# The node norm after the second aggregation: two staged functions become one with three row buffers

## The chip, the cores and the metric

The kernel runs on one core of one Trainium2 chip. The metric is the device time of one execution in microseconds, the median of several runs. The core has TensorE (PE, with its weight loads PEld), VectorE (DVE), ScalarE (ACT), GpSimd (POOL) and SyncE (SP), which only issues transfers here. DVE, ACT and GpSimd work on tiles of 128 partitions in SBUF; PE writes to PSUM.

## The reference

Four layers over 12500 nodes of 256 features: a graph layer, a feed-forward layer with eight experts, a second graph layer with a batch norm, and an attention that routes to four experts. The change touches the third, between the sum over edges and the attention's first product:

```python
def _L1_gnn_ref(x, A_indices, A_values, A_shape, W, bias, gamma, beta):
    h = jnp.einsum('nd,df->nf', x, W)
    row, col = (A_indices[0], A_indices[1])
    gathered = A_values[:, None] * h[col]
    agg = jax.ops.segment_sum(gathered, row, num_segments=A_shape)
    h = agg + bias
    mean = jnp.mean(h, axis=0)
    var = jnp.mean(jnp.square(h - mean), axis=0)
    h = (h - mean) * jax.lax.rsqrt(var + BN_EPS) * gamma + beta
    return jax.nn.relu(h)
...
    x = x + _L1_gnn_ref(_layernorm(x, axis=-1), edge_index, edge_weight, 12500, L1_gnn_W, L1_gnn_bias, L1_gnn_gamma, L1_gnn_beta)
    x = x + _L1_ffn_ref(_layernorm(x, axis=-1)[None], L1_ffn_W_gat, L1_ffn_att_src, L1_ffn_att_dst, L1_ffn_b_gat, L1_ffn_ln_gamma, L1_ffn_ln_beta, L1_ffn_W1, L1_ffn_b1, L1_ffn_W2, L1_ffn_b2, L1_ffn_edge_index)[0]
```

`_L1_ffn_ref` begins with `x_flat @ W_gat`, a product with 16 columns.

## The kernel before

The nodes are padded to 98 tiles of 128 rows (`TILES`), in 14 groups (`GROUPS`) of seven (`GROUP`); a group is an operand of 128x1792 numbers. The program is a row of stages. Each stage (`Stage`) has its own buffers and semaphores, in it every engine has its own list of instructions, and it ends with a barrier of all engines, so nothing of one stage runs beside another. Within a stage the engines are ordered by semaphores alone. `Chain` makes a DVE instruction wait for the one before it; where a stage is a loop (`Fori`), `hold` computes the awaited value in a register, which adds register instructions (L96) between the others.

After the second aggregation the sums over edges of all nodes lie in SBUF (`agg`). Two functions follow.

`node_statistics` (L1551) finds the mean and variance of each of the 256 features. PE sums the 98 tiles with a matrix of ones into `sum_ps` (L1579 to L1582, the middle ones in a loop), DVE makes the mean (L1615). DVE then writes `agg` minus the mean for a group into one of two buffers `dev` (L1622), ACT squares it in place (L1605), PE sums it into `sq_ps` (L1590), and DVE may use the buffer again when PE is done. Variance, root, reciprocal and the rows `gain` and `offset` follow (L1629 to L1638).

`update_nodes` (L805) with `kind="batch_norm"` makes, for each group, `part` = `agg` times `gain` (L987), plus `offset` (L988), and x + max(`part`, 0) (L989), all on DVE; then the layer norm of each row: `bn_stats` and `bn_aggr` for seven tiles (L992, L993), the root on ACT (L938), the reciprocal (L996), and the normalized rows `f` (L1003). SP loads the old rows x (L848) and stores the new x (L851) and f (L854). For each tile PE transposes f (L902), ACT copies the transposed tile back (L933), PE multiplies it with `gat_w` to 16 columns (L909, L910), and ACT copies them into `heads` (L949). A turn of the loop is two groups, with two buffers each for x and f. PE's list has, for each tile, the transposes and then the product of the same tile:

```python
for c in range(2):
    ins = nc.tensor.transpose(xt_ps[m % 2][:, c, :], src[:, c * P:(c + 1) * P], k.ident[:, :])
ins.then_inc(transposed, 1)
pe.wait_ge(used, used_value)
pe.wait_ge(turned, i * PT + m + 3)
```

SP issues both loads of a turn only after both f of the turn before are stored.

Other stages to which rows below belong: `layer_norm_in` (L148) is the first stage: layer norm of x on DVE (L188, L189, L201), a GpSimd addition of a broadcast row to a group (L208) that starts when the group's f are done, and PE's tail in which the transposes of the next tile precede the product of this one. `update_first` (L1012) is the update after the first aggregation, with the same order on PE; its product has 8 columns (L1082) and begins with a matmul for the bias (L1080); its transposes are L1070. `update_experts` (L1114) has three buffers for x; GpSimd clears a buffer there (L1175) and DVE makes f (L1208). In the experts' stage DVE sorts edges with comparisons of two inputs (L471, L472, L473), and GpSimd copies the payload (L491).

## Time and profile before

| | us |
|---|---|
| median of 3 runs | 8925.62 (8924.4 to 8925.65) |
| the profiled execution's own time | 8919.56 |
| its span | 8917.8 |
| node statistics, first PE instruction to the next stage's first load | 6661.83 to 6774.58 |
| node update, first load to the last ACT copy | 6774.58 to 7076.85 |

The profile gives the start, duration and engine of each instruction, and for an idle engine what ended its wait. Over the whole span PE is busy for 77%, DVE for 54%, ACT for 41%, GpSimd for 58%. Because of the barriers a stage is read by itself: what matters is what its engines do in its own window, and which wait ends last there.

### The profile page before, as it was taken

How to read it: one execution, taken by the hardware profiler on the slowest of the kernel's cores; microseconds unless marked ns; L12 is line 12 of the kernel's file. 1: busy time of each engine (PE TensorE's matmuls, PEld its weight loads, DVE VectorE, ACT ScalarE, POOL GpSimd, SP SyncE). 2: the span in 40 equal slices, each digit the busy share in tenths (PEclk: the TensorE clock that was granted, in tenths of full speed). 3: DMA queues.
4: the chain of work that ended last, by engine and by line, in shares of the span. 5: the costliest groups of instructions: out<-in, count | busy, mean ns of one | idle time of the engine just before them, and what ended most of it. 6: DMA issues, size and time to landing. Idle time of an engine off the chain costs nothing. (4 is left out here: it accounts for less than half of the span.)

```text
span 8917.8 us, 85432 instructions
## 1 busy us (share of the span) xinstructions
PE 6843.4 (77%) x22034; PEld 4303.5 (48%) x22034; DVE 4851.0 (54%) x8553; ACT 3689.7 (41%) x9689; POOL 5150.7 (58%) x4954
## 2 busy tenths in 40 slices
PE   5688888888882999974477777777776499999916
PEld 4333333333371666643233334443444388888815
DVE  5455555555545988717666666666655523232315
ACT  3466666666520222223355555555542133333303
POOL 3677777777705222114377777777760177777760
PEclk8555555555556999987667776666666599999968
DMA  4533333333334111115333333333332422222219
GB/s 139 158 101 100 102 102 101 102 102 101 98 116 135 43 48 52 39 62 159 94 96 97 96 97 97 97 96 96 96 89 83 125 63 69 67 66 65 68 24 343
DMA packets 557882, 865.24 MB, mean 97 GB/s; under 512 B 115953, under 2 KB 422596, under 8 KB 557106
## 3 DMA queue, kind: packets, MB, share of 16 engines
q0 software_dynamic: 210368, 480.82, 20.4%
q1 hardware_dynamic: 347062, 379.21, 12.9%
q8 instruction: 184, 3.01, 0.1%
q14 instruction: 268, 2.20, 0.1%
HBM read 641.91 MB, written 219.29 MB: 97 GB/s over the span
## 5 line engine op out<-in xcount | busy, mean ns | idle before, releaser
L718 PE MATMUL part<-rows,spread 128*128 128x256 f32 x6656 | 3374.5, 620 | 939.4 <-DMA rows<-h,row 313.1
L718 PEld LDWEIGHTS part<-rows,spread 128*128 128x128 f32 x6656 | 1544.9, 283 | 2652.2 <-issue 1732.7
L692 DVE TENSOR_TENSOR agg<-agg,part 128x256 f32 x3328 | 1401.5, 421 | 1762.9 <-PE part L718 1468.1
L675 POOL DMA_INDIRECT rows<-h,row x1664 | 1764.3, 1060 | 535.5 <-issue 494.4
L675 POOL DMA_INDIRECT rows<-f,row x1664 | 1661.7, 999 | 534.7 <-issue 498.1
L743 ACT ACTIVATE spread<-iota,place 128x128 f32<-128x128 f32 x3328 | 1017.8, 388 | 1998.5 <-PE part L718 1811.4
L1743 POOL DMA_INDIRECT rows<-gat,src x1122 | 1086.3, 968 | 341.9 <-issue 341.9
L749 ACT ACTIVATE spread<-spread,weight 128x128 f32<-128x128 f32 x3328 | 1017.4, 388 | 13.6
L1819 PE MATMUL hid_ps<-ft,w 128*128 128x256 f32 x3136 | 714.3, 380 | 18.7 <-ACT hid L1870 10.9
L1829 PE MATMUL y_ps<-w,hid 128*128 128x256 f32 x3136 | 708.7, 379 | 0.0
L1819 PEld LDWEIGHTS hid_ps<-ft,w 128*128 128x128 f32 x3136 | 592.6, 191 | 102.4 <-ACT hid L1870 15.8
L1870 ACT ACTIVATE hid<-hid_ps,b 128x256 f32<-128x256 f32 x784 | 324.1, 472 | 756.2 <-PE hid_ps L1819 755.7
L1829 PEld LDWEIGHTS y_ps<-w,hid 128*128 128x128 f32 x3136 | 595.8, 190 | 81.0
L1967 DVE TENSOR_TENSOR y<-y_ps,b 128x512 f32<-128x512 f32 x196 | 135.6, 692 | 850.8 <-PE y_ps L1829 848.7
L491 POOL COPY spare<-pay 128x1024 f32<-128x1024 f32 x93 | 196.9, 2117 | 694.8 <-DVE pay L478 450.4
L472 DVE TENSOR_TENSOR key<-key 128x1024 f32<-128x1024 f32 x342 | 486.7, 1423 | 5.9
L745 ACT ACTIVATE spread<-spread,ones 128x1024 f32<-128x1024 f32 x416 | 477.7, 1148 | 13.5
L1511 PE MATMUL y_ps<-w2s,hid 128*128 128x256 f32 x2048 | 476.2, 386 | 0.0
L1496 PE MATMUL hid_ps<-xt,w1s 128*128 128x512 f32 x1024 | 446.7, 594 | 3.3 <-DMA b2s<-in_L_ffn_b 3.3
L473 DVE TENSOR_TENSOR key<-key 128x1024 f32<-128x1024 f32 x342 | 419.1, 1225 | 11.7
L1511 PEld LDWEIGHTS y_ps<-w2s,hid 128*128 128x128 f32 x2048 | 378.5, 190 | 88.8 <-issue 32.5
L704 DVE TENSOR_TENSOR hot<-iota,fields 128x1280 bf16<-128x1280 f32 (+1 forms) x205 | 305.6, 1491 | 6.9
(373 smaller groups left out, 6228.1 us busy)
## 6 DMA issues: line engine op xcount, KB each, us to landing
x<-x SPq DMA_DIRECT2D x56, 896.0 KB, 8.9
expert_rows<-y SPq DMA_DIRECT2D x196, 256.0 KB
made<-expert_rows SPq DMA_DIRECT2D x14, 3584.0 KB
rows<-f,row POOLq DMA_INDIRECT x1664, 2.8
rows<-h,row POOLq DMA_INDIRECT x1664, 2.8
f<-f SPq DMA_DIRECT2D x28, 896.0 KB, 4.1
rows<-gat,src POOLq DMA_INDIRECT x1122
xbuf<-zero SPq DMA_DIRECT2D x128, 128.0 KB, 2.6
```

Source lines behind the costliest of these rows:

```text
L472: link(nc.vector.tensor_tensor(b[:, :, 0, :], a[:, :, 0, :], a[:, :, 1, :], ALU.min))
L675: pool.indirect_dma_start(out=rows[:, u, :], out_offset=None, in_=table, in_offset=bass.IndirectOffsetOnAxis(ap=q.row[:, p:p + 1], axis=0) ...
L692: nc.vector.tensor_tensor(sum_t, sum_t, part[:, p % NB, 0:D], ALU.add).then_inc(added, 1)
L718: nc.tensor.matmul(part[:, p % NB, 0:D], spread[:, p % (2 * BANKS), :], rows[:, u, :], start=True, stop=True).then_inc(multiplied, 1)
L743: nc.scalar.activation(spread[:, p % (2 * BANKS), :], k.iota[:, :], ACT.Square, bias=q.place[:, p:p + 1]).then_inc(squared, 1)
L745: nc.scalar.activation(spread[:, h, :], spread[:, h, :], ACT.Relu, scale=-1.0, bias=k.ones[:, 0:1]).then_inc(marked, 1)
L749: nc.scalar.activation(spread[:, p % (2 * BANKS), :], spread[:, p % (2 * BANKS), :], ACT.Copy, scale=q.weight[:, p:p + 1]).then_inc(spread ...
L1496: ins = nc.tensor.matmul(hid_ps[h % HB][:, :], w1s[n][:, c, fc * P:(fc + 1) * P], xt[g % 2][:, c, :], start=c == 0, stop=c == 1)
L1511: ins = nc.tensor.matmul(out, hid[g % 2][:, fc, q * P:(q + 1) * P], w2s[n][:, fc, :], start=False, stop=fc == FC - 1)
L1743: pool.indirect_dma_start(out=rows[b % 3][:, j, :], out_offset=None, in_=table, in_offset=at(src[:, b * B + j:b * B + j + 1])).then_inc(ga ...
L1819: ins = nc.tensor.matmul(hid_ps[m % 3][:, c, :], w1[:, e, d, fc * P:(fc + 1) * P], ft[k2 % 2][:, d, :], start=d == 0, stop=d == 1)
L1829: ins = nc.tensor.matmul(y_ps[n % 2][:, q, :], hid[n % 3][:, fc, q * P:(q + 1) * P], w2[:, n % GEXP, fc, :], start=fc == 0, stop=fc == FC - 1)
```

## The change

`node_statistics` and the batch-norm branch of `update_nodes` are replaced by one stage, `normalize_nodes`. (The named tuples `Routed` and `Normed` go too.)

- First sums: PE sums the tiles of the last seven groups, written out without a loop. DVE adds the first seven groups into one group `partial`, of which PE then sums the seven tiles.
- Centring: DVE adds minus the mean to `agg` in place, all 14 groups with no wait between. ACT squares into two buffers of its own, `square`.
- `offset` is gone: since `agg` is centred, a group's `part` is `agg` times `gain` plus beta. Both operations are GpSimd's now, into two buffers `part`; GpSimd starts group g when the sum of group g-2 is done.
- DVE keeps x + max(`part`, 0), the layer norm and f, and has the sum and moments of group g+1 ahead of the f of group g. The f aren't chained to each other.
- x has three buffers. SP loads the first two groups at the start of the stage, and group g+2 after it has stored x of group g; that load waits until f of group g-1 is done.
- PE has the transposes of tile t+1 ahead of the product of tile t, and ACT the copy of tile t+1 ahead of the result of tile t.
- All loops of these two functions are written out.

Of the removed functions the diff shows only the heads.

```diff
-def update_nodes(nc, k, head, x_old, x_new, f_new, w, width, bias, result):
...
-def node_statistics(nc, k, sums, gain, offset, params):
...
+def normalize_nodes(nc, k, sums, params, x_old, x_new, f_new, w, width, result):
...
+    group = lambda g: sums[:, g * GROUP:(g + 1) * GROUP, :]
+    B, HALVES = 3, GROUPS // 2
...
+        square = [s.sb(f"square{h}", [P, GROUP, D], F32) for h in range(2)]
+        part = [s.sb(f"part{h}", [P, GROUP, D], F32) for h in range(2)]
+        x = [s.sb(f"x{b}", [P, GROUP, D], F32) for b in range(B)]
+        f = [s.sb(f"f{b}", [P, GROUP, D], F32) for b in range(2)]
...
+                def load(g):
+                    if g >= B:
+
+                        sp.wait_ge(normed, (g - B + 1) * GROUP)
+                        sp.wait_ge(x_stored[g % B], g // B * 16)
+                    sp.dma_start(x[g % B][:, :, :], xo[g, :, :, :]).then_inc(loaded[g % B], 16)
+
+                load(0)
+                load(1)
+                for g in range(GROUPS):
+                    sp.wait_ge(summed, g + 1)
+                    sp.dma_start(xn[g, :, :, :], x[g % B][:, :, :]).then_inc(x_stored[g % B], 16)
+                    if g + 2 < GROUPS:
+                        load(g + 2)
+                    sp.wait_ge(normed, (g + 1) * GROUP)
+                    sp.dma_start(fn[g, :, :, :], f[g % 2][:, :, :]).then_inc(f_stored[g % 2], 16)
...
+                pool.wait_ge(weighed, 1)
+                for g in range(GROUPS):
+                    if g >= 2:
+                        pool.wait_ge(summed, g - 1)
+                    nc.gpsimd.tensor_tensor(part[g % 2][:, :, :], group(g), bc(gain[:, :], GROUP, 1), ALU.mult).then_inc(scaled, 1)
+                    pool.wait_ge(scaled, g + 1)
+                    nc.gpsimd.tensor_tensor(part[g % 2][:, :, :], part[g % 2][:, :, :], bc(beta_p[:, :], GROUP, 1), ALU.add).then_inc(parted, 1)
...
+                for t in range(HALVES * GROUP, TILES):
+                    nc.tensor.matmul(out, k.ones[:, :], sums[:, t, :], start=t == HALVES * GROUP, stop=False)
+                pe.wait_ge(added, HALVES - 1)
+                for j in range(GROUP):
+                    ins = nc.tensor.matmul(out, k.ones[:, :], partial[:, j, :], start=False, stop=j == GROUP - 1)
+                ins.then_inc(totalled, 1)
+                pe.wait_ge(masked, 1)
+                for g in range(GROUPS):
+                    pe.wait_ge(squared, g + 1)
+                    for j in range(GROUP):
+                        t = g * GROUP + j
+                        ins = nc.tensor.matmul(sq_ps[:, 0:D], (last if t == TILES - 1 else k.ones)[:, :], square[g % 2][:, j, :],
+                                               start=t == 0, stop=t == TILES - 1)
+                    ins.then_inc(used, 1)
...
+                for t in range(TILES):
+                    if t < TILES - 1:
+                        turn(t + 1)
+                    pe.wait_ge(copied, t + 1)
+                    if t >= 2:
+                        pe.wait_ge(made, t - 1)
+                    for c in range(2):
+                        ins = nc.tensor.matmul(out_ps[t % 2][:, 0:width], xt[t % 2][:, c, :], w[:, c, :], start=c == 0, stop=c == 1)
+                    ins.then_inc(multiplied, 1)
...
+                for g in range(GROUPS):
+                    act.wait_ge(centred, g + 1)
+                    if g >= 2:
+                        act.wait_ge(used, g - 1)
+                    nc.scalar.activation(square[g % 2][:, :, :], group(g), ACT.Square).then_inc(squared, 1)
+                act.wait_ge(all_squared, 1)
...
+                for g in range(1, HALVES):
+                    if g > 1:
+                        dve.wait_ge(added, g - 1)
+                    nc.vector.tensor_tensor(partial[:, :, :], group(0) if g == 1 else partial[:, :, :], group(g), ALU.add).then_inc(added, 1)
+                dve.wait_ge(totalled, 1)
+                dve.wait_ge(params_in, 48)
+                link(nc.vector.tensor_tensor(mean[:, :], mean[:, :], bias_p[:, :], ALU.add))
+                link(nc.vector.tensor_tensor(mean[:, :], bias_p[:, :], mean[:, :], ALU.subtract))
+                for g in range(GROUPS):
+                    nc.vector.tensor_tensor(group(g), group(g), bc(mean[:, :], GROUP, 1), ALU.add).then_inc(centred, 1)
+                dve.wait_ge(used, GROUPS)
+                dve.sem_inc(all_squared, 1)
+                dve.wait_ge(rooted, 1)
+                link(nc.vector.tensor_tensor(gain[:, :], std[:, :], gamma_p[:, :], ALU.mult))
+                dve.sem_inc(weighed, 1)
+                def add(g):
+                    xg = x[g % B][:, :, :]
+                    dve.wait_ge(parted, g + 1)
+                    dve.wait_ge(loaded[g % B], (g // B + 1) * 16)
+                    link(nc.vector.scalar_tensor_tensor(xg, part[g % 2][:, :, :], 0.0, xg, ALU.max, ALU.add))
+                    dve.sem_inc(summed, 1)
+                    for j in range(GROUP):
+                        link(nc.vector.bn_stats(stats[:, j, :], x[g % B][:, j, :]))
+                        link(nc.vector.bn_aggr(mv[:, g % 2, j, :], stats[:, j, :]))
+                    dve.sem_inc(var_done, 1)
+                add(0)
+                for g in range(GROUPS):
+                    if g < GROUPS - 1:
+                        add(g + 1)
+                    dve.wait_ge(std_done, g + 1)
+                    link(nc.vector.reciprocal(rstd[:, g % 2, :], row_std[:, g % 2, :]))
+                    if g >= 2:
+                        dve.wait_ge(turned, (g - 1) * GROUP)
+                        dve.wait_ge(f_stored[g % 2], g // 2 * 16)
+                    for j in range(GROUP):
+                        nc.vector.tensor_scalar(f[g % 2][:, j, :], x[g % B][:, j, :], mv[:, g % 2, j, 0:1], rstd[:, g % 2, j:j + 1],
+                                                ALU.subtract, ALU.mult).then_inc(normed, 1)
...
-                with Stage(nc) as s2:
-                    gain, offset = s2.sb("gain", [P, D], F32), s2.sb("offset", [P, D], F32)
-                    node_statistics(nc, k, agg, gain, offset, (a["L1_gnn_bias"], a["L1_gnn_gamma"], a["L1_gnn_beta"]))
-                    update_nodes(nc, k, Normed(kind="batch_norm", sums=agg, gain=gain, offset=offset), x2, x3, f3,
-                                 k.gat_w, W, None, heads)
+                normalize_nodes(nc, k, agg, (a["L1_gnn_bias"], a["L1_gnn_gamma"], a["L1_gnn_beta"]), x2, x3, f3, k.gat_w, W, heads)
```

DVE in the update, a group in the middle. Before (x0, part and f0 are the buffers of x, of the scaled sums and of f; rows that repeat are left out, as are the register instructions between):

```order
L987 TENSOR_TENSOR part_81796<-agg1_46842,gain_81566 128x1792
L988 TENSOR_TENSOR part_81796<-part_81796,offset_81567 128x1792
L989 SCALAR_TENSOR_TENSOR x0_81792<-part_81796,x0_81792 128x1792
L992 BN_STATS stats_81799<-x0_81792 128x6
L993 BN_AGGR mv_81800<-stats_81799 128x2
...
L996 RECIPROCAL rstd_81802<-std_81801 128x7
L1003 TENSOR_SCALAR f0_81794<-x0_81792,mv_81800,rstd_81802 128x256 x7
```

Now:

```order
L1507 SCALAR_TENSOR_TENSOR x1_81580<-part1_81578,x1_81580 128x1792
L1510 BN_STATS stats_81586<-x1_81580 128x6
L1511 BN_AGGR mv_81587<-stats_81586 128x2
...
L1519 RECIPROCAL rstd_81589<-row_std_81588 128x7
L1524 TENSOR_SCALAR f0_81582<-x0_81579,mv_81587,rstd_81589 128x256 x7
```

The two tensor_tensor have left DVE, and between the sum of group 1 (x1) and the next sum stand the f of group 0. GpSimd, which had one instruction in these two functions, has this row of them now (`last` is the mask for the padding):

```order
L1400 AFFINE_SELECT last_81573<-ones 128x128
L1407 TENSOR_TENSOR part0_81577<-agg1_46842,gain_81569 128x1792
L1409 TENSOR_TENSOR part0_81577<-part0_81577,beta_p_81572 128x1792
L1407 TENSOR_TENSOR part1_81578<-agg1_46842,gain_81569 128x1792
L1409 TENSOR_TENSOR part1_81578<-part1_81578,beta_p_81572 128x1792
```

The moved operations alternate between two buffers, 28 in all. PE at the start of the tail. Before, transposes (`xt_ps`) and products (`tail_ps`) of the same tile alternate:

```order
L902 MATMUL xt_ps0_81803<-ident,f0_81794 128x128 x2
L906 REGISTER_ALU
L909 MATMUL tail_ps0_81805<-gat_w,xt0_81797 128x16
L910 MATMUL tail_ps0_81805<-gat_w,xt0_81797 128x16
L899 REGISTER_ALU
```

Now:

```order
L1434 MATMUL xt_ps1_81593<-ident,f0_81582 128x128 x2
L1445 MATMUL out_ps0_81594<-gat_w,xt0_81584 128x16 x2
L1434 MATMUL xt_ps0_81592<-ident,f0_81582 128x128 x2
L1445 MATMUL out_ps1_81595<-gat_w,xt1_81585 128x16 x2
```

The transposes into one buffer stand ahead of the product from the other.

## Rows read from the trace of the kernel before

**Rows 1.** Windows: us, busy us (x instructions) of each engine, clock, DMA share, GB/s.
```profile
6661.00:6711.00 50.00, 49.17 (x196) 32.98 (x196) 0.00 (x0) 0.00 (x0) 0.29 (x1) 0.95 0.03 8
6852.00:7078.00 226.00, 120.58 (x462) 88.55 (x462) 137.06 (x257) 46.76 (x164) 0.00 (x0) 0.50 0.39 126
```

**Rows 2.** Timeline: start us, us, engine line op out<-in, idle before; the statistics.
```profile
6661.83 1.22 PE L1579 MATMUL sum_ps<-agg,ones 128*128 128x256 f32 x2 [5.07 <-ACTq L1601]
...
6711.28 0.42 DVE L1615 TENSOR_SCALAR mean<-sum_ps 128x256 f32<-128x256 f32 x1 [53.75 <-PE sum_ps L1582]
...
6768.34 0.42 DVE L1629 TENSOR_SCALAR var<-sq_ps 128x256 f32<-128x256 f32 x1 [5.11 <-PE sq_ps L1590]
...
6771.18 0.42 DVE L1633 TENSOR_TENSOR gain<-std,row 128x256 f32<-128x256 f32 x1
6771.64 0.42 DVE L1635 TENSOR_TENSOR mean<-mean,row 128x256 f32<-128x256 f32 x1
```

**Rows 3.** Timeline, squares of the deviations: PE after a pause, PE later, ACT.
```profile
6715.64 8.60 PE L1590 MATMUL sq_ps<-dev,ones 128*128 128x256 f32 x28 [4.50 <-ACT dev L1605]
...
6732.60 6.33 PE L1590 MATMUL sq_ps<-dev,ones 128*128 128x256 f32 x28 [1.01 <-ACT dev L1605]
...
6733.90 1.70 ACT L1605 ACTIVATE dev<-dev 128x1792 f32<-128x1792 f32 x1 [1.34 <-DVE dev L1622]
```

**Rows 4.** Timeline of the node update: two loads awaited, and its last instruction.
```profile
6822.12 2.02 DVE L987 TENSOR_TENSOR part<-agg,gain 128x1792 f32<-128x1792 f32 x1 [8.81 <-DMA x<-x]
...
7031.91 2.03 DVE L987 TENSOR_TENSOR part<-agg,gain 128x1792 f32<-128x1792 f32 x1 [8.87 <-DMA x<-x]
...
7076.67 0.18 ACT L949 ACTIVATE heads<-tail_ps 128x16 f32 x1 [1.27 <-PE tail_ps L910]
```

**Rows 5.** Groups by line, the update: count, busy us, mean ns, idle.
```profile
L989 DVE SCALAR_TENSOR_TENSOR x<-part,x 128x1792 f32<-128x1792 f32 x14 | 28.4, 2025 | 1.5
```

**Rows 6.** Layer norm of the first stage: DVE's timeline; GpSimd's line, ns min/median/max.
```profile
24.60 0.43 DVE L188 BATCH_NORM_STATS2 stats<-agg 128x6 f32<-128x256 f32 x1
...
25.28 0.43 DVE L188 BATCH_NORM_STATS2 stats<-agg 128x6 f32<-128x256 f32 x1
...
105.18 2.35 DVE L201 TENSOR_SCALAR f<-agg,mv,rstd 128x256 f32<-128x256 f32 x7
...
L208 POOL TENSOR_TENSOR agg<-agg,b x14: 3977/3982/3997, 36.3 to 145.6; 128x1792 f32<-128x1792 f32 x14
```

**Rows 7.** Timeline while the experts' stage sorts: DVE with two inputs, GpSimd's copy.
```profile
2904.91 1.23 DVE L471 TENSOR_TENSOR mask<-key 128x1024 uint16<-128x1024 f32 x1
2904.94 2.10 POOL L491 COPY spare<-pay 128x1024 f32<-128x1024 f32 x1 [5.07 <-DVE pay L478]
2906.17 1.94 DVE L472 TENSOR_TENSOR key<-key 128x1024 f32<-128x1024 f32 x1
```

**Rows 8.** Timeline of the second node update: a GpSimd memset meets DVE's f.
```profile
4024.45 1.60 POOL L1175 MEMSET clean<- 128x1792 f32 x1
...
4025.12 3.13 DVE L1208 TENSOR_SCALAR f<-x,mv,rstd 128x256 f32<-128x256 f32 x7
```

**Rows 9.** First node update: PE's timeline for one tile, and a window.
```profile
2467.35 0.67 PE L1070 MATMUL xt_ps<-ident,f 128*128 128x128 f32 x2
2467.94 0.59 PE L1080 MATMUL out_ps<-gate_b,ones 1*128 1x8 f32 x2
2468.47 1.02 PE L1082 MATMUL out_ps<-gate_w,xt 128*128 128x8 f32 x4
2469.34 0.67 PE L1070 MATMUL xt_ps<-ident,f 128*128 128x128 f32 x2
...
2466.00:2640.00 174.00, 174.00 (x699) 143.07 (x699) 81.35 (x267) 51.44 (x187) 0.00 (x0) 0.50 0.41 138
```

**Rows 10.** SP's queue in the node update: a store of f, then two loads.
```profile
6813.44 0.37 SPq L854 DMA_DIRECT2D f<-f  x1
6814.36 1.89 SPq L848 DMA_DIRECT2D x<-x  x2
```

More of the change, by code:

```diff
@@ L38 @@
 Pairs = namedtuple("Pairs", "row place weight tile")
-Routed = namedtuple("Routed", "kind table rows scale")
-Normed = namedtuple("Normed", "kind sums gain offset")
 Tally = namedtuple("Tally", "fields counts words")
@@ L1575, in _ @@
             @block.tensor
             def _(pe):
-                pe.wait_ge(go, 1)
                 out = sum_ps[:, 0:D]
-                nc.tensor.matmul(out, k.ones[:, :], sums[:, 0, :], start=True, stop=False)
-                with pe.Fori(1, TILES - 1) as t:
-                    nc.tensor.matmul(out, k.ones[:, :], sums[:, bass.ds(t, 1), :].rearrange("p o d -> p (o d)"), start=False, stop=False)
-                nc.tensor.matmul(out, k.ones[:, :], sums[:, TILES - 1, :], start=False, stop=True).then_inc(summed, 1)
@@ L1583, in _ @@
-                pe.wait_ge(mask_done, 1)
-                def turn(i, first, end):
-                    for h in range(2):
-                        pe.wait_ge(squared, i * 2 + h + 1)
-                        for j in range(GROUP):
-                            is_last = end and h == 1 and j == GROUP - 1
-                            ins = nc.tensor.matmul(sq_ps[:, 0:D], (last if is_last else k.ones)[:, :], dev[h][:, j, :],
-                                                   start=first and h == 0 and j == 0, stop=is_last)
-                        ins.then_inc(used, 1)
@@ new lines, in _, with root, turn @@
+                act.wait_ge(all_squared, 1)
+                nc.scalar.activation(std[:, :], var[:, :], ACT.Sqrt, bias=k.eps[:, :]).then_inc(rooted, 1)
+                def root(g):
+                    act.wait_ge(var_done, g + 1)
+                    nc.scalar.activation(row_std[:, g % 2, :], mv[:, g % 2, :, 1], ACT.Sqrt, bias=k.eps[:, :]).then_inc(std_done, 1)
+                def turn(t):
+                    act.wait_ge(turned, t + 1)
+                    if t >= 2:
+                        act.wait_ge(multiplied, t - 1)
+                    nc.scalar.activation(xt[t % 2][:, :, :], xt_ps[t % 2][:, :, :], ACT.Copy).then_inc(copied, 1)
@@ new lines, in _ @@
+                root(0)
+                root(1)
+                turn(0)
+                for t in range(TILES):
+                    g, j = t // GROUP, t % GROUP
+                    if t < TILES - 1:
+                        turn(t + 1)
+                    if j == 3 and 2 <= g + 1 < GROUPS:
+                        root(g + 1)
+                    act.wait_ge(multiplied, t + 1)
+                    nc.scalar.activation(result[:, t, :], out_ps[t % 2][:, 0:width], ACT.Copy).then_inc(made, 1)
@@ L1611, in _ @@
                 link = Chain(dve, chain)
-                dve.wait_ge(go, 1)
-                dve.wait_ge(loaded, 48)
-                dve.wait_ge(summed, 1)
-                link(nc.vector.tensor_scalar(mean[:, :], sum_ps[:, 0:D], 1.0 / N, None, ALU.mult))
-                def turn(i, again):
-                    for h in range(2):
-                        if again:
-                            hold(dve, go, used, i * 2 + h - 1)
-                        nc.vector.tensor_tensor(dev[h][:, :, :], sums[:, bass.ds((i * 2 + h) * GROUP, GROUP), :], bc(mean[:, :], GROUP, 1),
-                                                ALU.subtract).then_inc(dev_done, 1)
@@ L1631, in _ @@
-                dve.wait_ge(std_done, 1)
+                dve.sem_inc(all_squared, 1)
+                dve.wait_ge(rooted, 1)
                 link(nc.vector.reciprocal(std[:, :], std[:, :]))
-                link(nc.vector.tensor_tensor(gain[:, :], std[:, :], rows[1][:, :], ALU.mult))
-                link(nc.vector.tensor_tensor(mean[:, :], mean[:, :], rows[0][:, :], ALU.add))
-                link(nc.vector.tensor_tensor(tmp[:, :], rows[0][:, :], mean[:, :], ALU.subtract))
-                link(nc.vector.tensor_tensor(tmp[:, :], tmp[:, :], gain[:, :], ALU.mult))
@@ L1638, in _ @@
-                link(nc.vector.tensor_tensor(offset[:, :], tmp[:, :], rows[2][:, :], ALU.add))
+                link(nc.vector.tensor_tensor(gain[:, :], std[:, :], gamma_p[:, :], ALU.mult))
[10 more added lines that the diff above has]
+                    dve.sem_inc(var_done, 1)
```

236 lines of the change are left out of this document (32 added, 204 removed).

## Prediction

> **What bounds the kernel now.** The change stays inside one stretch of the program, from the start of the node statistics at 6661.8 us to the last copy of the node update at 7076.85 us, 415.0 us of a span of 8917.8. The stages are divided by barriers on all engines, so what ends this stretch earlier ends the kernel earlier, one for one. I first read the windows [rows 1]: in the statistics PE is busy nearly all the time; in the update PE is busy 120.6 of 226 us and DVE 137.1, DMA 0.39: nothing is full, so there a chain of waits is the bound. The timeline gives its dates [rows 2]: first sums from 6661.83 until the mean starts at 6711.28 (49.4 us), squares until 6768.3, and the norm's gain is ready at 6771.60, which I call the hand-over: 109.8 us after the start. From there the update takes 305.2 us: two groups of seven tiles take (7031.91 - 6822.12) / 5 = 42.0 us, in which DVE does all the arithmetic of each group in turn, and sits 8.8 us waiting for rows that are loaded only when both buffers are free [rows 4].
>
> **The statistics.** The first sums were 98 tiles of two passes at 49.4 / 196 = 0.25 us a pass, in a loop. The same passes written out run faster in the squares: 28 of them in 6.33 us, from which I take the last one's 0.38 and a wait of 0.15: 5.80 / 27 = 0.215 us. The first 28 after a pause take 8.60 us, 2.3 more, with the clock still at its lower level [rows 3]. The change leaves 49 tiles and 7 tiles of partial sums, 112 passes: 112 x 0.215 + 2.3 = 26.4 us. DVE's six additions (2.03 us for the shape [rows 5], and 0.04 for the wait: two chained steps of 0.42 us start 0.46 apart [rows 2]) take 12.4 us from the same start and are hidden behind the 49 tiles (21 us). If that cover failed the cost would be small, since only the last 3 us of PE's work wait for them.
> Then DVE makes mean and minus mean (0.15 + three steps of 0.46 = 1.5), centres one group (2.03), ACT squares it (1.70 [rows 3] + 0.05): PE starts at 26.4 + 5.3 = 31.7. Before, DVE waited for PE to free one of two buffers and a pair of groups took 7.3 us; now all centring goes in place without a wait and PE is the bound: 196 x 0.215 + 2.3 + 0.5 of small waits = 44.9, so 76.6. Variance, root, reciprocal and gain take 6771.60 - 6768.34 = 3.3 us as before [rows 2]: hand-over at 80.0 us instead of 109.8, a **gain of 29.8 us**. The bounds are 27 (PE's first start and the in-place centring a little slower) and 32 (no cold start in the first sums).
>
> **The update, by engine.** Four later steps on small rows disappear behind the hand-over, as do a barrier and the first load, which now comes during the statistics. A group then costs:
> DVE: one scalar_tensor_tensor of 128x1792, 2.03 + 0.04; seven pairs of bn_stats and bn_aggr, which follow at 0.68 us in the first stage's layer norm (its chain is written without the register waits) [rows 6], 4.75; reciprocal 0.3; seven f at 2.35 together: 9.45 us.
> GpSimd: multiply and add, both 128x1792. The trace has such an add beside DVE's bn_stats: 3.98 us, 14 times between 3.977 and 3.997 [rows 6]. With a wait between and one before: 8.09 us. No row shows a multiply of two tiles on GpSimd; I take the add's time, since shape and operands are the same; lower bound 3.0, upper bound 6 us.
> PE: the tail for a tile is two transposes and four passes with 16 columns. The update of the first layer has the same pipelined order, 8 columns and one more matmul; there PE is busy for 174.00 of 174 us, with the clock at 0.50, and a tile is transposes 0.59, extra matmul 0.53, four passes 0.87 [rows 9]. Without the extra one 1.46 us a tile, 10.2 us a group; I take the lower clock level, since that stage kept it though PE never paused.
> DMA: f store, x store and the load of the next but one group are now issued together. Three such transfers were issued from 6813.44 on [rows 10]; the second was in place when DVE went on at 6822.12 [rows 4], 8.7 us later, and for the third I add 1.3: about 10 us; the loaded rows are needed one period after the burst.
>
> **Which of them sets the period.** Added one by one none would exceed 10.2. But the trace shows DVE and GpSimd shutting each other out. GpSimd's copy and DVE's comparison with two inputs start 0.03 us apart, the copy lasts 2.10 us, and DVE's next two-input operation lasts 1.94 instead of 1.23: it ends 1.07 us after the copy, which is its 1024 elements with nothing before them [rows 7]. An f that meets a GpSimd memset waits too: a group of f lasts 3.13 us instead of the 2.35 of rows 6 and ends 2.2 us after the memset [rows 8]. bn_stats and bn_aggr aren't held up, nor do they hold up GpSimd [rows 6, 8]. So both of GpSimd's operations exclude the scalar_tensor_tensor and the seven f, and only bn and reciprocal (5.05 us) go beside them. GpSimd may begin part(k+2) only after the sum of group k. Then: 8.09 us of GpSimd with bn under it, f 2.2 after it (they wait some 3 us), then the next sum 2.07: **12.4 us a group**. PE's 10.2 and the loads' 10 lie under it.
> The Trainium skill bears on this in two places. SBUF — State Buffer, section "SBUF: two separate sides", calls the shared port pair "an exclusive lock, not a bandwidth split" for a DVE operation with two SBUF inputs or in its two-port mode against a GpSimd operation that reads SBUF; rows 7 and 8 agree, but no row has a scalar_tensor_tensor against a GpSimd tensor_tensor, and by the rule they exclude each other as well. GPSIMD Engine Reference, section "Engine selection", sends element-wise work to VectorE, which speaks against this change: left on DVE, the two operations would give 9.45 + 4.1 = 13.6 us a group, so by these rows the move still gains 1.2.
>
> **The sum of the update.** Start: GpSimd's first part ends 8.1 us after the hand-over, and nothing makes GpSimd wait before part 1's multiply, so I let the first sum end at 14.1, the second at 24.1 (each held up by one operation), the third at 40.5. Ten periods of 12.4 follow: 164.5. The last sum has no GpSimd work before it: 9.4, so 173.9. PE began group 10 13.3 us before that and then has 28 tiles at 1.46, ending 27.6 after; with the last copy 28.2. Together 202.1 instead of 305.2: a **gain of 103.1 us**. End of the stretch at 80.0 + 202.1 = 282.1 instead of 415.0; in all 132.9, say 133 us. The profiled execution took 8919.6 (span 8917.8, 1.8 around it): 8787 and span 8785. The median lies 6 us above it: 8925.6 - 133 = **8793 us**. All other stages keep code and data.
>
> **Rivals.**
> A. The two-tile operations don't shut each other out after all (or only briefly). Then PE's tail is the bound: the first f at 23.2 us after the hand-over, 98 x 1.46 = 143.1, last copy 0.6: 167 instead of 202, time 8793 - 35 = **8758**. For it: the pairs in question are in no row. Against it: two kinds of pairs that are.
> B. The exclusion costs more: GpSimd's multiply is 6 us instead of 4, or GpSimd gets in between two f and DVE waits twice. Period 14.4, 12 of them count: + 24, **8817**. For it: f are issued without waits, and nothing reserves the port for all seven. Against: GpSimd is out of work by then.
> C. Slower than before. The multiply would have to be so long that it eats all: 133 / 13 = 10.2 us more, so 14.2 us, 3.6 times the add. Up to there GpSimd hides nothing and every microsecond counts 13 times. At 20 us: 8793 + 13 x 16 = **9001**. Only an operation that GpSimd does in a wholly different way would do that; nothing in the rows points to it.
> D. It doesn't do what it says: each sum waits for its load, and stores and load follow each other so slowly that a group takes about the 21 us of before. Then only the statistics and the first load are gained: **8885**, still faster. Against it: the loads have 12.4 us for 10.
>
> **How the numbers follow.** Forecast 8793 (own range 8778 to 8806): 0.60. A 0.17, B 0.18, D 0.02, C 0.02, and 0.01 for no visible change. 8793 is the likeliest case's. The range takes in A and B: 8748 (A with the statistics' best bound and a PE a little faster in the tail) to 8822. About 0.2%, 18 us, is what a measurement of this kernel can tell from no change; every case but C and the last is faster by more: faster 0.97, same 0.01, slower 0.02.
>
> **What would show it.** Statistics: first sums in one run of 26 us, squares without gaps, hand-over near 80 us. Update: scalar_tensor_tensor on DVE at a distance of 12.4 us, GpSimd's operations 3.98 us, the first f of each group starting when GpSimd's add ends, and lasting longer than 0.41. A distance of 10.2 with PE never idle speaks for A, GpSimd operations of 5 us and more for B. The clock in the update at 0.50; were it at 1.0, PE's last 28 tiles would take up to half the time, and the kernel up to 14 us less. The prediction is wrong if the sum waits for its load (DMA x), or if GpSimd's operations don't touch DVE's at all.

## The result and the profile after

| | before | after |
|---|---|---|
| median, us (runs) | 8925.01 (4: 8915.02 to 8925.65) | 8777.52 (4: 8774.87 to 8782.68) |
| ratio, 95% interval | | 0.9837 [0.9825, 0.9849] |
| profiled execution, us (its span) | 8919.6 (8917.8) | 8777.8 (8776.0) |
| mean granted clock of PE | | 0.733 |
| the stretch: start of the statistics to the last copy of the update, us | 415.0 | 275.0 |

The kernel became 147.5 us faster, where 8793 (132.6 faster than the runs shown then) had been predicted; the measured time lies in the range and is 15.5 us below the forecast. Of the 141.8 us between the two spans 140.0 lie in the stretch. The stage starts 2.5 us later than before and what follows it takes 4.3 us less; the code of those parts is the same.

Two other views of the stage, first the windows: us from and to, length, busy us (x instructions) of PE, PE's weight loads, DVE, ACT and GpSimd, granted clock, DMA share, GB/s. The first two answer to the statistics in [rows 1], the third to the update there.

```profile
6662.00:6692.00 30.00, 26.84 (x112) 22.98 (x112) 13.05 (x8) 0.00 (x0) 0.29 (x1) 0.88 0.23 75
6698.00:6741.00 43.00, 42.70 (x194) 37.14 (x192) 22.02 (x13) 20.62 (x13) 0.00 (x0) 0.98 0.00 1
6780.00:6911.00 131.00, 90.77 (x456) 89.58 (x454) 121.94 (x251) 44.92 (x162) 79.38 (x20) 0.50 0.73 226
```

In the squares PE now runs without a gap. In the update PE is busy 91 of 131 us, GpSimd 79 and DVE 122, and DVE's busy time contains its waiting for GpSimd, as the timeline shows below. The DMA share went from 0.39 to 0.73: the same rows in less time.

The timeline of PE in the statistics (start us, us, engine line operation, idle before), which answers to [rows 2, 3]:

```profile
6664.32 23.81 PE L1415 MATMUL sum_ps<-agg,ones 128*128 128x256 f32 x98 [5.10 <-PEq L70]
6687.97 3.19 PE L1418 MATMUL sum_ps<-partial,ones 128*128 128x256 f32 x14
6696.47 43.80 PE L1425 MATMUL sq_ps<-square,ones 128*128 128x256 f32 x194 [5.31 <-ACT square L1454]
```

The first sums are one run of 26.9 us, the partial sums follow without a wait, and the squares are one run of 43.8 us, with two last passes behind it. The gain is ready at 6743.99 (its operation starts at 6743.57 and takes 0.42), 79.7 us after the start.

The timeline of DVE, GpSimd and SP for one period of the update, which has no counterpart before, since there DVE did all of it alone:

```profile
6842.55 2.01 DVE L1507 SCALAR_TENSOR_TENSOR x<-part,x 128x1792 f32<-128x1792 f32 x1
6842.66 0.36 SPq L1391 DMA_DIRECT2D f<-f  x1
6843.06 0.72 SPq L1387 DMA_DIRECT2D x<-x  x1
6843.88 1.39 SPq L1381 DMA_DIRECT2D x<-x  x1
6844.70 3.99 POOL L1407 TENSOR_TENSOR part<-agg,gain 128x1792 f32<-128x1792 f32 x1 [4.16 <-DVEq L1508]
6848.77 3.96 POOL L1409 TENSOR_TENSOR part<-part,beta_p 128x1792 f32<-128x1792 f32 x1
6849.57 0.20 DVE L1519 RECIPROCAL rstd<-row_std 128x7 f32<-128x7 f32 x1
6849.81 5.00 DVE L1524 TENSOR_SCALAR f<-x,mv,rstd 128x256 f32<-128x256 f32 x7
6854.73 2.01 DVE L1507 SCALAR_TENSOR_TENSOR x<-part,x 128x1792 f32<-128x1792 f32 x1
```

GpSimd starts 2.15 us after the sum starts, its two operations end at 6852.73, and the seven f, which take 2.35 us when nothing holds them up, end at 6854.81: 2.08 us after GpSimd. 2.15 + 8.03 + 2.00 (from GpSimd's end to the next sum) = 12.18 us, the distance of the two sums. The answer for the tile f between 6840 and 6870 has the durations of single f (ns, minimum, median, maximum of 21):

```profile
L1524 DVE TENSOR_SCALAR f<-x,mv,rstd x21: 400/403/3065, 6837.6 to 6866.6; 128x256 f32<-128x256 f32 x21
```

One long f of 3.07 us accounts for the whole difference between 5.00 and 2.35, and it is the first of its group: 6849.81 + 3.07 is 6852.88, just behind GpSimd's end at 6852.73. The wait shows as a longer duration, not as a late start.

### The profile page after: what moved, and what is told of

It reads as the page before. It is cut to its first block and busy times, and to the rows that moved or that the text cites. A ratio compares the mean times of both kernels' runs of the same rounds, so it can differ in the third digit from the quotient of the medians.

```text
span 8776.0 us, 83571 instructions
## 1 busy us (share of the span) xinstructions
PE 6792.9 (77%) x21950; PEld 4303.2 (49%) x21950; DVE 4835.4 (55%) x8529; ACT 3686.7 (42%) x9689; POOL 5263.6 (60%) x4982
## 5 line engine op out<-in xcount | busy, mean ns | idle before, releaser
L1287 PEld LDWEIGHTS hid_ps<-xt,w1s 128*128 128x128 f32 x1024 | 195.7, 191 | 234.6 <-issue 233.0
```

What stands on the lines that cost most here:

```text
L1287: ins = nc.tensor.matmul(hid_ps[h % HB][:, :], w1s[n][:, c, fc * P:(fc + 1) * P], xt[g % 2][:, c, :], start=c == 0, stop=c == 1)
```

## The experiments

Dates are counted from the start of the stage. The changed kernel has: hand-over 79.7, first sum starts at 87.9, last at 249.6, end of the stage 275.0; distances of the sums 10.9 and 18.0 at first, then 12.17 to 12.19 with one of 12.8, and 10.45 for the last. The chip of the first four runs took 10344.1 us for the kernel before, with other stages longer, while the durations inside this stage were those above; there I compare stages, not totals. Unless the text says otherwise, the theory in an expectation is that of the prediction.

**dve_scale.** Both scaling operations go back to DVE.

```diff
-                    dve.wait_ge(parted, g + 1)
+                    link(nc.vector.tensor_tensor(part[g % 2][:, :, :], group(g), bc(gain[:, :], GROUP, 1), ALU.mult))
+                    link(nc.vector.tensor_tensor(part[g % 2][:, :, :], part[g % 2][:, :, :], bc(beta_p[:, :], GROUP, 1), ALU.add))
```

> The changed kernel with both scaling operations (agg times gain, plus beta) back on DVE, ahead of the sum; GpSimd has nothing to do in the update. In the changed kernel sums on DVE are 12.18 us apart and the stage lasts 275.0 us from its start to the last ACT copy. Theory (GpSimd and DVE shut each other out, so the move only hides 5 of 8 us under bn_stats and costs the f their place): f takes 2.35 us a group again instead of 5.0, distance 7.1 + 2.35 + 2 x 2.07 = 13.6; the start is 8 us shorter; stage about 284 us. Rival (the loads set the distance of 12.2): distance stays 12.2 and the stage is some 8 us shorter, 267. Rival (the move to GpSimd hides all of its 4.1 us): distance 16.3, stage about 310.

Total 10213.0. Hand-over 80.7, first distance 11.2, then 13.64 to 13.66 with one of 13.9, end 285.5. DVE's timeline of one period:

```profile
7239.53 2.03 DVE L1500 SCALAR_TENSOR_TENSOR x<-part,x 128x1792 f32<-128x1792 f32 x1
...
7246.81 2.35 DVE L1517 TENSOR_SCALAR f<-x,mv,rstd 128x256 f32<-128x256 f32 x7
7249.07 2.03 DVE L1497 TENSOR_TENSOR part<-agg,gain 128x1792 f32<-128x1792 f32 x1
7251.13 2.02 DVE L1498 TENSOR_TENSOR part<-part,beta_p 128x1792 f32<-128x1792 f32 x1
7253.19 2.03 DVE L1500 SCALAR_TENSOR_TENSOR x<-part,x 128x1792 f32<-128x1792 f32 x1
```

With GpSimd silent the seven f take 2.35 us. The move to GpSimd takes 4.1 us of work off DVE in each group but gains only 13.65 - 12.18 = 1.47 a group: the rest goes into the wait of f. At the end of the stage it has gained 10.5 us. At the start it costs 8.0 (the third sum starts 37.1 us after the hand-over instead of 29.1), the later distances bring 17.5, and 1.0 is a later hand-over in this run.

**two_bufs.** x has two buffers instead of three.

```diff
-    B, HALVES = 3, GROUPS // 2
+    B, HALVES = 2, GROUPS // 2
```

> The changed kernel with two buffers of x instead of three, all else the same. A load can then start only when f of the group two before is done, and the next sum waits for it. Theory: the load's 5.3 us comes on top: f done 10.3 us after a sum, load 5.3, sum 2.0, distance 17.6, stage 275 + 11 x 5.4 = 335. Rival (the third buffer hides nothing, since GpSimd sets the distance): distance 12.2, 275. Rival (store and load share the queue, the load takes 10): distance 22, stage 385.

Total 10291.0, distance 18.0 to 19.6 (the third sum comes after 24.2, the last after 15.5), end 348.3: the third buffer is worth 73 us, more than half of what the whole change brings. That is nearest to the theory and 13 us over it, in part because DVE goes on 5.8 to 7.3 us after a load is issued, where 5.3 had been expected. DVE's timeline and SP's:

```profile
...
7266.80 2.03 DVE L1507 SCALAR_TENSOR_TENSOR x<-part,x 128x1792 f32<-128x1792 f32 x1 [5.89 <-DMA x<-x]
```
```profile
7260.93 0.36 SPq L1381 DMA_DIRECT2D x<-x  x1
7261.33 0.56 SPq L1391 DMA_DIRECT2D f<-f  x1
...
```

A group's sum now waits for a load that is issued only when the f before it are done. Here SP issues this load (L1381) ahead of the stores of f and x, and DVE goes on 5.9 us later. I come back to that.

**sums_on_pe.** PE sums all 98 tiles of the first sums, DVE adds nothing.

```diff
-                for t in range(HALVES * GROUP, TILES):
-                    nc.tensor.matmul(out, k.ones[:, :], sums[:, t, :], start=t == HALVES * GROUP, stop=False)
...
+                for t in range(TILES):
+                    ins = nc.tensor.matmul(out, k.ones[:, :], sums[:, t, :], start=t == 0, stop=t == TILES - 1)
```

> The changed kernel with all 98 tiles of the first sums on PE, none on DVE. Theory: 42 more tiles of two passes at 0.214 us: hand-over (gain ready) 17.9 us later, at 97.6 us after the stage's start instead of 79.7, stage 293. Rival (PE's passes are slowed by DVE's additions in the same SBUF rows, or the wait for them costs): passes faster without them, less than 14 us later. Rival (the gain was in writing the loop out): still the larger part of the gain, 49.4 down to 42.5, is there without DVE.

Total 10223.1. The mean starts at 44.0 instead of 26.9, the hand-over is at 97.5 and the end at 292.1: 17.2 us later, as the theory said. DVE's half of the first sums is worth those 17 us, and writing the loop out 49.4 - 44.0 = 5.4.

**wait_squares.** DVE's centring waits, as before, until PE has summed the squares of the group before the last.

```diff
+                    if g >= 2:
+                        dve.wait_ge(used, g - 1)
```

> The changed kernel where DVE centres group g only when PE has summed the squares of group g-2, as before. Theory (the free run of the centring lets PE run without gaps): PE has gaps of some 1 us in every pair again, squares take 52 instead of 44.2 us, hand-over 8 us later, stage 283. Rival (the gain in the squares came from ACT having buffers of its own, not from centring ahead): ACT can still be one group ahead, PE without gaps, no change within 1 us.

Total 10216.5. The hand-over is 6.6 us later (8 expected) and the end 7.0 us later, at 282.0; the squares fall into seven runs. Two rows of PE's timeline:

```profile
7126.74 6.31 PE L1425 MATMUL sq_ps<-square,ones 128*128 128x256 f32 x28 [0.82 <-ACT square L1454]
7133.87 6.31 PE L1425 MATMUL sq_ps<-square,ones 128*128 128x256 f32 x28 [0.82 <-ACT square L1454]
```

So four terms of the change are sized, each undone alone: 73 us for the third buffer, 17 for DVE's half of the sums, 11 for GpSimd, 7 for centring without waiting for PE. The new order of PE's and ACT's lists, the sum of group g+1 ahead of the f of group g on DVE, and the f that aren't chained were not undone. What they bring is not shown, nor that the terms add up: the four make 108 of the 140 us.

**no_beta.** GpSimd's addition of beta is left out (the kernel then computes `agg` times `gain` without beta), so that GpSimd has one operation a group. This tells exclusion apart from a plain GpSimd bound.

```diff
-                    nc.gpsimd.tensor_tensor(part[g % 2][:, :, :], group(g), bc(gain[:, :], GROUP, 1), ALU.mult).then_inc(scaled, 1)
-                    pool.wait_ge(scaled, g + 1)
-                    nc.gpsimd.tensor_tensor(part[g % 2][:, :, :], part[g % 2][:, :, :], bc(beta_p[:, :], GROUP, 1), ALU.add).then_inc(parted, 1)
+                    nc.gpsimd.tensor_tensor(part[g % 2][:, :, :], group(g), bc(gain[:, :], GROUP, 1), ALU.mult).then_inc(parted, 1)
```

> The changed kernel without GpSimd's addition of beta (left out of the computation): GpSimd has one operation of 4.0 us a group instead of two. Theory (exclusion sets the distance of 12.18): the multiply now lies wholly beside bn_stats, f takes 2.35 us again, no sum is lengthened; DVE would allow 9.45, but the loads need some 11.5 us from f to landing, and two distances must hold a load and a group: (11.5 + 9.45) / 2 = 10.5, with DVE waiting for DMA x. Rival (semaphore round trips between GpSimd and DVE, not the port, set it): 12.18 - 4.0 = 8.2 and no f is shortened. Rival (PE's tail or the loads set 12.18 already): distance 12.2, f still 5.0.

Total 8741.8 (before, same chip: 8917.5). The stage ends at 243.3; distances 9.5 to 11.6, mean 10.3, where 10.5 had been expected. The row of a group's f and of the sum behind it:

```profile
6814.34 2.35 DVE L1522 TENSOR_SCALAR f<-x,mv,rstd 128x256 f32<-128x256 f32 x7
6817.79 2.02 DVE L1505 SCALAR_TENSOR_TENSOR x<-part,x 128x1792 f32<-128x1792 f32 x1 [1.10 <-DMA x<-x]
```

A GpSimd operation of 3.98 us fits under the bn operations of the same group (4.75 us), and no f waits. Where nothing else intervenes the distance is 9.53, DVE's own work; in six groups the load now comes last (7.6 us together).

**beta_on_dve.** GpSimd multiplies, DVE adds beta.

```diff
                     dve.wait_ge(parted, g + 1)
+                    link(nc.vector.tensor_tensor(part[g % 2][:, :, :], part[g % 2][:, :, :], bc(beta_p[:, :], GROUP, 1), ALU.add))
```

> The changed kernel with beta added on DVE (ahead of the sum), the multiply on GpSimd; complete. Theory: DVE 2 x 2.07 + 4.75 + 0.3 + 2.35 = 11.5 us a group, GpSimd's 4.0 wholly beside bn_stats: distance 11.5 (from 12.18), start 6 us shorter (first part after 4 + 2 us, no operation held up by the second), stage 275 - 6 - 7 = 262. Rival (moving work back to DVE costs what it costs, 2.07 a group, since f was not really held up): distance 14.2.

Total 8771.0, first distance 9.1 and then 11.58 or 11.59 throughout, end 263.2, 11.8 us earlier than in the changed kernel; 6.4 of them are there at the third sum, counted from the hand-over. DVE's timeline, and GpSimd's operation beside it:

```profile
6845.11 2.02 DVE L1506 SCALAR_TENSOR_TENSOR x<-part,x 128x1792 f32<-128x1792 f32 x1
...
6852.38 2.35 DVE L1523 TENSOR_SCALAR f<-x,mv,rstd 128x256 f32<-128x256 f32 x7
6854.65 2.01 DVE L1504 TENSOR_TENSOR part<-part,beta_p 128x1792 f32<-128x1792 f32 x1
6856.69 2.03 DVE L1506 SCALAR_TENSOR_TENSOR x<-part,x 128x1792 f32<-128x1792 f32 x1
```
```profile
6847.27 3.98 POOL L1407 TENSOR_TENSOR part<-agg,gain 128x1792 f32<-128x1792 f32 x1 [7.60 <-DVEq L1507]
```

GpSimd ends at 6851.25, before f starts. The 2.05 us that DVE now spends on beta replace 2.65 us of waiting.

**beta_on_dve_timed.** The same kernel, run more often.

> beta_on_dve again, timed. Its stage lasted 263.3 us, 11.7 less than the changed kernel's 275.0. Theory: all of that reaches the kernel's time, so against before about 148 + 12 = 160 us, ratio 0.982, and nothing is given back in later stages. Rival: within the scatter of 5 us no difference from the changed kernel (0.9837).

8768.64 us (8755.14 to 8773.99) against 8922.88, ratio 0.983 [0.9816, 0.9843]. It beats the kernel before. Against the changed kernel the 11.5 us are there in the stage of both profiles (263.2 and 263.5), but the intervals of the two ratios overlap, so the totals don't show it.

**extra_row.** Each tile's product gets one more matmul of a single row, as in `update_first` [rows 9].

```diff
+                    nc.tensor.matmul(out_ps[t % 2][:, 0:width], k.ones[0:1, :], k.zero[0:1, 0:width], start=True, stop=False)
                     for c in range(2):
-                        ins = nc.tensor.matmul(out_ps[t % 2][:, 0:width], xt[t % 2][:, c, :], w[:, c, :], start=c == 0, stop=c == 1)
+                        ins = nc.tensor.matmul(out_ps[t % 2][:, 0:width], xt[t % 2][:, c, :], w[:, c, :], start=False, stop=c == 1)
```

> The changed kernel with one more matmul for each tile in PE's tail, one row of ones by a row of zeros (it adds nothing), as the first update has it for its bias. A tile takes 1.17 us in the changed kernel and 1.99 in the first update with this matmul. Theory (the matmul costs its neighbours too, 0.82 in all): 1.99 a tile, 13.9 a group, so PE sets the distance: about 13.9, stage some 35 us longer. Rival (it costs its own 0.53 alone, and the rest lies in the first update's stage): 1.70 a tile, 11.9 a group, distance stays 12.18, only the last tiles are later by 8 to 11 us.

Total 8820.7; after the first two, as in the changed kernel, the distance is 12.17 or 12.18 up to the sixth sum and then 13.98 to 14.05, with PE without a pause; end 311.9, 36.9 us later, so the theory held. PE's timeline of a tile here, and then of a tile of the changed kernel:

```profile
6855.12 0.67 PE L1434 MATMUL xt_ps<-ident,f 128*128 128x128 f32 x2
6855.72 0.60 PE L1444 MATMUL out_ps<-zero,ones 1*128 1x16 f32 x2
6856.26 1.03 PE L1446 MATMUL out_ps<-gat_w,xt 128*128 128x16 f32 x4
6857.13 0.67 PE L1434 MATMUL xt_ps<-ident,f 128*128 128x128 f32 x2
```
```profile
6933.38 0.67 PE L1434 MATMUL xt_ps<-ident,f 128*128 128x128 f32 x2
6933.84 0.88 PE L1445 MATMUL out_ps<-gat_w,xt 128*128 128x16 f32 x4
6934.55 0.67 PE L1434 MATMUL xt_ps<-ident,f 128*128 128x128 f32 x2
```

2.01 us a tile against 1.17, both at a granted clock of 0.50, the lower of its two levels. Between its start and the product's the extra matmul takes 0.54, but the transposes take 0.60 instead of 0.46 up to the next start and the product 0.87 instead of 0.71: it costs 0.84 us, 0.30 of them in its neighbours.

**f_on_act.** ACT makes f (x times `rstd` plus a `shift` that DVE makes with one small operation), so that DVE has nothing left that GpSimd could hold up but the sum.

```diff
+                    link(nc.vector.scalar_tensor_tensor(shift[:, g % 2, :], mv[:, g % 2, :, 0], -1.0, rstd[:, g % 2, :], ALU.mult, ALU.mult))
+                    dve.sem_inc(shifted, 1)
...
+                    nc.scalar.activation(f[g % 2][:, j, :], x[g % B][:, j, :], ACT.Identity, bias=shift[:, g % 2, j:j + 1],
+                                         scale=rstd[:, g % 2, j:j + 1]).then_inc(normed, 1)
```

> The changed kernel with f made by ACT (x times the reciprocal plus a shift that DVE makes for the group) instead of DVE. Theory: the port then carries 8.09 of GpSimd, the shift (0.25) and the sum (2.07): distance 10.4. Rival (f were not what waits; DVE just has less work): 12.18 - 2.35 = 9.8. Rival (PE and ACT become the bound, since ACT has f, copy and result for every tile): 7 x 1.6 = 11.2 or more, PE waiting for ACT.

Missed: 8799.6, distances 13.7 to 14.6 from the fourth sum on, end 296.4. DVE's timeline, GpSimd's, and SP's store of the f:

```profile
6833.19 2.03 DVE L1523 SCALAR_TENSOR_TENSOR x<-part,x 128x1792 f32<-128x1792 f32 x1 [4.15 <-DMA x<-x]
...
6840.46 2.93 DVE L1536 SCALAR_TENSOR_TENSOR shift<-mv,rstd 128x7 f32<-128x7 f32 x1
...
6861.70 2.02 DVE L1523 SCALAR_TENSOR_TENSOR x<-part,x 128x1792 f32<-128x1792 f32 x1 [4.40 <-DMA x<-x]
```
```profile
6839.41 3.96 POOL L1411 TENSOR_TENSOR part<-part,beta_p 128x1792 f32<-128x1792 f32 x1
```
```profile
6850.92 0.36 SPq L1393 DMA_DIRECT2D f<-f  x1
```

The shift, seven columns wide, has two inputs and ends at 6843.39, when GpSimd ends (6843.37). ACT, which does f between its copies for PE, has the seven done 7.5 us later. Only then does SP store f and issue a load. From the sum at 6833.19 to the sum at 6861.70, which waits for that load, two groups pass: 7.3 + 2.9 + 7.5 + 10.8 = 28.5, so 14.25 a group.

**f_act_beta_dve.** Both at once: f on ACT, beta on DVE.

> f on ACT and beta on DVE together; complete. Theory: DVE 2 x 2.07 + 4.75 + 0.5 = 9.4 us, GpSimd 4.0 beside bn_stats, then the loads (three transfers a group, some 8 us of full rate) or ACT with PE (7 x 1.3 = 9.1) are next: distance 9.5 to 10.5, stage about 245. Rival (ACT is the bound): 11.2 or more.

Missed: 8774.2, distances of 9.6 to 10.8 and 14.7 to 15.3 in turn after a first of 9.1, end 276.2; DVE waits 37.0 us for rows of x. The shift is no longer held up (0.17 us), but the loop of loads stays.

**f_act_beta_dve_x4.** The theory then was that the load waits for its buffer. The same with four buffers for x.

```diff
-    B, HALVES = 3, GROUPS // 2
+    B, HALVES = 4, GROUPS // 2
```

> f on ACT, beta on DVE, and four buffers of x. With three, distances alternated between 10 and 15 us and DVE waited 37 us for DMA x, since f on ACT is finished late and its x buffer is free late. Theory: with a fourth buffer the wait is gone, DVE's 9.5 sets the distance, first sum 9 us after the hand-over: stage about 80 + 9 + 13 x 9.7 + 26 = 241. Rival (the queue itself is full: three transfers of 0.9 MB a group at what the shorter distances need): distance 11 and more, DMA waits stay.

That theory fell: 8787.2 (8786.6 to 8787.9), ratio 0.9849 [0.9834, 0.9864], end 277.8, and much the same alternation. Groups by line, DVE's sum, with three buffers and with four:

```profile
L1522 DVE SCALAR_TENSOR_TENSOR x<-part,x 128x1792 f32<-128x1792 f32 x14 | 28.4, 2025 | 37.1 <-DMA x<-x 37.0
```
```profile
L1522 DVE SCALAR_TENSOR_TENSOR x<-part,x 128x1792 f32<-128x1792 f32 x14 | 28.4, 2026 | 37.3 <-DMA x<-x 37.2
```

SP's timeline with four buffers shows why:

```profile
6814.73 0.36 SPq L1393 DMA_DIRECT2D f<-f  x1
6815.14 0.56 SPq L1389 DMA_DIRECT2D x<-x  x1
6815.80 1.28 SPq L1383 DMA_DIRECT2D x<-x  x1
```

The load goes out 1.07 us after the store of f, as with three buffers. In SP's list the load of group g+3 stands behind the store of the f of group g, and it is that place that holds it, not the buffer. With three buffers the loop is: sum, bn and shift 7.4 us, f on ACT 7.5, stores and load 10.9, sum of the group after next: 25.8 us, which is one short and one long distance (10.75 + 15.08).

**no_beta_x4.** Four buffers, with GpSimd's addition left out again.

> The kernel without beta (left out of the computation), with four buffers of x. With three its distances scattered between 9.5 and 11.6 with 7.6 us of waits for DMA x. Theory (the load was late only because its buffer was free late): distance 9.53 throughout, stage some 8 us shorter than 243.4. Rival (the transfers' rate is the limit): waits for DMA x remain, distance stays near 10.3.

8743.5, end 243.9 (243.3 with three buffers), waits for x 8.5 us (7.6): again the fourth buffer changes nothing. Two things remain that would shorten this loop: to issue the load ahead of the stores (in two_bufs, where it is ahead, DVE goes on 5.8 to 7.3 us after it is issued; behind the stores it was 8.6 to 11.6 in no_beta, f_on_act, f_act_beta_dve and the two kernels with four buffers, wherever DVE waited), or ahead of the wait for f. Neither was tried, so how much belongs to the list and how much to the transfers stays open.

## Why the prediction was right, step by step

**The statistics.** First sums 26.4 predicted, 26.9 measured; squares start at 31.7, measured 32.2; hand-over 80.0, measured 79.7. The squares themselves, from PE's start to the variance, took 44.3 us where 44.9 had been predicted. DVE's additions are hidden, as said (they end 12.5 us after the start), and every term is right within 0.6 us.

**GpSimd's multiply**, which no row of before had: 3.95 to 3.99 us, the same as the addition in [rows 6]. The lower bound 3.0 and the upper 6 both fell away, with them the first half of rival B, and rival C.

**The exclusion** is the step on which the sum turned, and it held. Rival A (10.2 a group, 8758) falls by the 5.00 us of f above and by no_beta, where f takes 2.35 again. The start shows it for the pair that no row had before. DVE's and GpSimd's timeline from the hand-over on, where [rows 7, 8] had other pairs:

```profile
6752.15 3.95 POOL L1407 TENSOR_TENSOR part<-agg,gain 128x1792 f32<-128x1792 f32 x1
6752.23 5.76 DVE L1507 SCALAR_TENSOR_TENSOR x<-part,x 128x1792 f32<-128x1792 f32 x1 [8.23 <-POOL part L1409]
6756.19 5.62 POOL L1409 TENSOR_TENSOR part<-part,beta_p 128x1792 f32<-128x1792 f32 x1
...
6765.81 5.62 POOL L1409 TENSOR_TENSOR part<-part,beta_p 128x1792 f32<-128x1792 f32 x1
6771.39 3.95 POOL L1407 TENSOR_TENSOR part<-agg,gain 128x1792 f32<-128x1792 f32 x1
6772.85 8.29 DVE L1524 TENSOR_SCALAR f<-x,mv,rstd 128x256 f32<-128x256 f32 x7
6775.42 3.96 POOL L1409 TENSOR_TENSOR part<-part,beta_p 128x1792 f32<-128x1792 f32 x1
```

The first sum starts 0.08 us after the multiply, lasts 5.76 us instead of 2.02 and ends 1.89 us after it; the addition behind it lasts 5.62 instead of 3.95 and ends 3.8 us after the sum: each waits until the other's operation is over. This is what the Trainium skill calls an exclusive lock (SBUF — State Buffer, section "SBUF: two separate sides"); the prediction had to carry the rule over to this pair, and the trace agrees. Rival B's second mechanism, GpSimd getting in between two f, exists too: the first group of f (8.29 us) is held up by the multiply, and again by the addition that starts behind it. But it does so only in this first group, where GpSimd still runs ahead; later GpSimd waits for the sum, as was argued against B. That bn_stats and bn_aggr are free of it had been read from [rows 6, 8], where no bn row stands beside a GpSimd operation; it holds: beside GpSimd's multiply they take 0.43 and 0.18 us, as alone. Of the signs that were named, the distance and GpSimd's 3.98 us came, but the first f doesn't start when GpSimd's addition ends: it starts 2.9 us before that and ends just behind it.

**The sums.** Their ends after the hand-over: predicted 14.1, 24.1, 40.5; measured 14.0, 23.6, 39.1. Ten periods of 12.4 were to follow; they took 122.4 us, 12.2 each, since GpSimd's two operations and the wait between them are 8.03, not 8.09, and the hand-overs a little shorter. The last distance was 10.45 instead of 9.4, for two reasons: 0.85 us of waiting for rows of x, and 0.2 of small waits. The last sum ends at 171.9 after the hand-over, 173.9 predicted.

**The loads.** About 10 us from the stores to the rows in place was predicted, against 12.4 that they have. It is nearer to the edge than that: where DVE waited in the changed kernel, it went on 12.7 us after the first of the three was issued (6805.50 to 6818.19) and 10.4 us after it (6903.54 to 6913.89), and over all variants whose load stands behind the stores it was 10.2 to 12.7. The two waits of the changed kernel are 1.4 us in all, so the term cost little here; it costs the variants with a shorter period more.

**The tail on PE** is the term that was mis-sized. From the end of the last sum to the end of the stage 28.2 us were predicted and 23.4 measured: 4.8 of the 7.1 us by which the stage is shorter than forecast (282.1 against 275.0). The step that failed is "without the extra one 1.46 us a tile": 0.53 was taken off the tile of [rows 9] for the extra matmul, and it costs 0.84 (extra_row). At 1.17 us a tile PE needs 8.2 us for a group, not 10.2, and does not lag behind DVE at all. PE's timeline before the f of the last groups but two and but one:

```profile
6911.16 0.69 PE L1434 MATMUL xt_ps<-ident,f 128*128 128x128 f32 x2 [1.13 <-DVE f L1524]
...
6921.63 0.69 PE L1434 MATMUL xt_ps<-ident,f 128*128 128x128 f32 x2 [2.07 <-DVE f L1524]
```

PE stands idle both times until DVE's f comes. So what follows the last sum is 5.7 us until the f of the last group but one, 14 tiles of 1.17 = 16.4, and 1.3 for the last product and copy; the forecast had PE working through 28 tiles of 1.46 without a pause. Of the 4.8 us, 1.0 is only that the last sum came late (PE began group 10 14.3 us before its end, not 13.3); 3.8 are the price of the tile. The granted clock stayed at 0.50, the lower level, as assumed; the sum's bound for it wasn't needed. The last f start 4.14 us late, for ACT's root, which stands behind the fourth tile of the group before; PE has work meanwhile, and nothing is lost.

**The miss of 15.5 us** is then: stage 7.1 (0.3 hand-over, 2.0 sums, 4.8 tail), 1.8 outside the stage in this pair of profiles, 6.3 because the profiled execution of before lay 6.0 below its median and the one of after 0.3 above it, and 0.3 of rounding. The mechanism was right, then, and not only the number: no two large errors cancel in it, and the one term that was clearly off, PE's tile, lies behind the last sum and not in the period. Only the stage's part is explained; the rest is within what a measurement of this kernel scatters.

## What to carry to other kernels

Where two engines shut each other out, don't ask how much work is moved but what lies beside it: one GpSimd operation of 3.98 us under 4.75 us of bn operations cost nothing, a second one gave back 2.65 of the 4.1 us that both took off DVE, and moving only the multiply was worth twice as much (stage 263.2) as moving both (275.0 against 285.5 with neither). Where the period of a pipeline shrinks, look for the loop that runs through the store queue: a load behind a store waits for what the store waits for, and a fourth buffer changed nothing here, twice. And don't price an instruction by subtracting its own row from a stage that has one more: take the distance of two starts in a stage that is as similar as can be, and keep the neighbours' change in the range.

## What was not expected of the hardware

- A matmul of a single row between matmuls of 128 costs more than its own row: 0.54 us of its own and 0.30 in the transposes and the product beside it, at a granted clock of 0.50.
- A DVE operation with two inputs of 128x7, 0.17 us long, is held up by GpSimd like a large one: in f_on_act it took 2.93 us in the median of 14 rows, where f_act_beta_dve has 0.17. Its small size did not spare it.
- GpSimd is held up by DVE too: its addition takes 5.62 us instead of 3.96 when DVE's sum is under way.
- DVE goes on 5.8 to 7.3 us after a load of x is issued ahead of two stores (eleven of twelve rows have at most 6.1), and 7.6 to 11.6 us after it where it is issued behind them (two_bufs: 7260.93 to 7266.80; changed kernel: 6906.34 to 6913.89 and 6806.57 to 6818.19).
